# Weighing all edge chunks ahead of the slice softmax in a graph-attention gather loop, one core

## What is computed

```python
xn = layernorm(x)
h  = xn @ W.T + b                                   # graph attention
v  = leaky_relu(a1[src] + a2[dst])                  # one score an edge
ev = exp(v - segment_max(v, src)[src])
gnn = segment_sum((ev / segment_sum(ev, src)[src])[:, None] * h[dst], src)
mix = linear_attention(xn)                          # q / normaliser @ (k^T v) @ wo + bo
x = x + gnn + mix
y = layernorm(x)
sw = softmax((y @ W_x + b_x) @ W_slice / temp)      # 8 heads x 64 slices, a row a node
tok = sw^T @ (y @ W_fx + b_fx), normalised; attention over the 64 slice tokens
out = x + (attention output spread back by sw) @ W_out + b_out
```

## Time and profile before

| | us |
|---|---|
| median of 3 runs | 1620.71 |
| lowest and highest run | 1609.23, 1620.91 |
| span of the profiled execution, first to last instruction | 2306.1 |

### The profile page before, as it was taken

How to read it: one execution, slowest core, us unless ns; L and a number is a source line. 1 busy time by engine, 2 the same in 40 slices (tenths; PEclk the granted TensorE clock), 3 DMA queues, 4 the chain that set the end, 5 groups by cost and what they waited for, 6 DMA issues and landing times. The chain is left out here.

```text
span 2306.1 us, 27679 instructions
## 1 busy us (share of the span) xinstructions
PE 1454.6 (63%) x8420; PEld 1093.9 (47%) x8420; DVE 1270.9 (55%) x4043; ACT 677.9 (29%) x1884; POOL 1004.7 (44%) x1126
## 2 busy tenths in 40 slices
PE   5599995355745655655655656656646547465889
PEld 3477874234534434434434434434434435344667
DVE  8978783154644644644644545545545535445744
ACT  0243441042322322322322323323323323223310
POOL 1167676535445445445345345345344354453000
PEclk8799997577778877778878778778777777787999
DMA  8011213223223223223223222222232232221064
GB/s 178 29 47 48 62 50 90 71 58 88 70 70 87 69 69 86 69 73 84 68 73 83 68 76 80 68 77 79 65 83 77 62 87 68 69 77 55 14 193 153
DMA packets 112593, 177.17 MB, mean 77 GB/s; under 512 B 35998, under 2 KB 84509, under 8 KB 112445
## 3 DMA queue, kind: packets, MB, share of 16 engines
q0 software_dynamic: 43184, 109.96, 18.0%
q1 hardware_dynamic: 52847, 44.64, 7.5%
q10 hardware_dynamic: 16414, 20.81, 2.9%
HBM read 139.68 MB, written 35.65 MB: 76 GB/s over the span
## 5 line engine op out<-in xcount | busy, mean ns | idle before, releaser
L1134 POOL DMA_INDIRECT big<-node_table,rest x825 | 784.9, 951 | 239.9 <-issue 225.9
L1220 PE MATMUL psum<-big 128*125 128x257 f32 x1700 | 399.2, 388 | 39.4 <-DVE big L1757 39.1
L1220 PEld LDWEIGHTS psum<-big 128*125 128x125 f32 x1700 | 316.2, 191 | 93.9 <-DVE big L1757 46.1
L1575 DVE TENSOR_SCALAR rest<-psum,rest 128x125 f32<-128x125 f32 x100 | 30.1, 344 | 594.8 <-remote 554.1
L1239 PE MATMUL psum<-rest 65*125 65x512 bf16 x52 | 34.6, 666 | 488.6 <-ACT big L1376 488.6
L1132 POOL TENSOR_TENSOR rest<-rest 1x1 f32<-1x1 f32 x100 | 18.9, 189 | 693.7 <-PE psum L1220 668.0
L1370 ACT ACTIVATE rest<-big,rest 128x125 f32<-128x125 bf16 x850 | 268.9, 493 | 134.2 <-DVE rest L1705 134.2
L1239 PEld LDWEIGHTS psum<-rest 65*125 65x125 bf16 x52 | 9.2, 176 | 521.2 <-ACT big L1376 521.0
L1376 ACT COPY big<-psum 128x250 f32<-128x250 f32 x52 | 19.1, 367 | 687.1 <-remote 682.5
L1241 PE MATMUL psum<-rest,big 128*125 128x512 f32 x208 | 177.5, 1005 | 0.0
L1757 DVE TENSOR_SCALAR big<-big,rest 128x125 f32<-128x125 bf16 x850 | 169.0, 281 | 0.0
(11 more groups left out here) (430 smaller groups left out, 2786.7 us busy)
## 6 DMA issues: line engine op xcount, KB each, us to landing
big<-node_table,rest POOLq DMA_INDIRECT x825
slice_weights<-rest ACTq DMA_DIRECT2D x51, 252.0 KB
big<-slice_weights SPq DMA_DIRECT2D x50, 252.0 KB, 3.8
node_table<-big SPq DMA_DIRECT2D x50, 126.0 KB
normalised_turned<-big SPq DMA_DIRECT2D x50, 125.0 KB
rest<-normalised_turned SPq DMA_DIRECT2D x50, 125.0 KB
out_dram<-rest ACTq DMA_DIRECT2D x50, 125.0 KB
X<-in_x_dram SPq DMA_DIRECT2D x1, 5600.0 KB
```

The lines of the kernel that those rows point to most:

```text
L1134: pool.indirect_dma_start(Gt[:, u, q * TW:(q + 1) * TW], None, table, bass.IndirectOffsetOnAxis(ap=item[:, u, 2 * q:2 * q + 1], axis=0)).t ...
L1220: mm = pe.matmul(bank[bAgg][0:R, 0:D + 1], P[:, u, q, :], Gt[:, at, q * TW:q * TW + D + 1], start=q == 0, stop=q == Q - 1)
```

## The change

TensorE's step calls `sum_edges` once for all five groups of chunks; the two groups that stood behind `turn_weights` (5 of the 17 chunks) move ahead of `turn_inverse`. VectorE's `add_sums` is split into `take_sums` (the instruction that reads PSUM) and `invert_sums` (the three small ones). `weigh` moves ahead of `soft_below`, and `invert_sums` moves behind `inverse_norms`. Nothing else changes: the same instructions run, and ScalarE's and GpSimd's programs are as before.

```diff
@@ TensorE step @@
-                        sum_edges(i, u, odd, GROUPS[:3])
+                        sum_edges(i, u, odd, GROUPS)
                         turn_inverse(i + 1)
                         turn_weights(i)
-                        sum_edges(i, u, odd, GROUPS[3:])
                         spread_inverse(i + 1)
@@ VectorE @@
-                    def add_sums(i, done, count):
+                    def take_sums(i, done, count):
 
                         dve.wait_ge(done, count)
                         dve.scalar_tensor_tensor(AGG, AGG, keepf, bank[bAgg][0:R, 0:D + 1], ALU.mult,
                                                  ALU.add).then_inc(s_agg, 1)
+
+                    def invert_sums(i):
+
                         dve.wait_ge(s_agg, SA * i + 1)
                         dve.tensor_scalar(sinv, AGG[:, D:D + 1], 1e-30, None, ALU.max).then_inc(s_agg, 1)
@@ VectorE step @@
-                        add_sums(i, used[(u - 1) % U], n + 1 if u == 0 else n + 2)
+                        take_sums(i, used[(u - 1) % U], n + 1 if u == 0 else n + 2)
+                        weigh(i, u)
                         soft_below(i)
-                        weigh(i, u)
                         inverse_norms(i + 1, ahead)
+                        invert_sums(i)
                         if ahead:
                             scores(following_j, following_k, 1)
@@ VectorE, after the loop @@
-                    add_sums(last, used[(TAIL - 1) % U], 2 * more + (TAIL - 1) // U + 2)
+                    take_sums(last, used[(TAIL - 1) % U], 2 * more + (TAIL - 1) // U + 2)
+                    invert_sums(last)
```

## The result

| | us |
|---|---|
| changed kernel, median of 4 (lowest, highest) | 1745.69 (1745.15, 1745.94) |
| kernel before, median of 4 | 1616.43 (1609.23, 1620.91) |
| ratio, with 95% interval | 1.0815 [1.0769, 1.0862] |
| predicted | 1699, range 1631 to 1750 |

Slower, as forecast, and inside the range, but by 129 us where the sum had 78. The profiled execution of the changed kernel has a span of 1744.2 us, what the timed runs have. The profile of before had 2306.1.

The account below looks back on a forecast made before the run. No engine is full; a chain through several engines, about 20.5 us a step with GpSimd's gathers level, bounds the kernel. VectorE's 2.75 us delay less TensorE's 1.08, say 1.6 x 49 = 78 us, gives 1620.7 + 78 = 1699 us, range 1631 to 1750.

Parts of the forecast that it names:

- the sum: Whole loop: L1202 comes 1.7 and 1.5 us later, say 1.6, in each of 49 steps, 78 us.
- The wait at L1565: VectorE stands idle 2.7 us before L1565 for ScalarE's copies behind the late exponential; L1565 moves from 8.72 to 11.0.
- TensorE's series: TensorE's 34 matmuls, 7.8 us, run as one series from about 5 to about 13; L1202 then follows L1712 at once.
- Set-up and end taken over from the first profile: Set-up 474.3 us and end 143.0 us assumed equal in timed runs, leaving a 1003 us loop, 20.5 us a step.
- the hand-made 20.2 and 20.9: Clean step before the change: 20.2 us from the first step, 20.9 from the other with sums at 5.47; mean 20.5.
- its upper bound: Top of the range, 1750 us; all of VectorE's delay reaching the end was put at 49 x 2.75 = 135 us.
- Two signs that did not come: In the profile after: last L1742 intervals, without gathers, about 22.5 us; profiled span may move little, steps ending with gathers.
- 1, TensorE as the bound: Faster: the sums' earlier start wins up to 1.4 us a step, 69 us, giving 1552 us; chance 0.09.
- 2, another engine's pace: GpSimd's 20.5 us sets the pace and hides some delay: 1684 us, or 1631 at most for no change; chance 0.13.
- 3: Full delay: VectorE's small instructions ahead of `spread` late too, 1.1 us more; 49 x 2.75, 1756 us; chance 0.10.

Follow-up runs that it names:

- the run with the copies ahead: Changed kernel with ScalarE's three copies of the transposed marks moved ahead of the slice exponential: 1591.0 us, ratio to before 0.985.
- VectorE's part alone: Changed kernel with TensorE's sums put back into two series, the last five chunks behind the turning of the weights: 1815.3 us, ratio 1.122.
- the faster versions: Changed kernel with ScalarE's copies ahead of the exponential, 1591.0 us; that plus 3 filling matmuls, 1592.3; kernel before with 4 filling matmuls, 1591.9.
- TensorE's part alone: Kernel before with all 17 chunks summed ahead of the turning of the weights, VectorE's order as before: 1744.5 us in three runs, 1714.9 in the fourth.

## Why the prediction was right, and where it was short

- **The wait at L1565**: right within a tenth. Idle 2.7 us forecast, 2.74 measured; L1565's successor at 11.0 and 11.03; L1705's at 11.8 and 11.77; L1712's at 14.9 and 14.90; L1202 at 17.3 and 17.33. That the copies behind the exponential are the cause is shown by the run with the copies ahead, which takes it away.
- **TensorE's series**: "start at about 5 and are done by about 13", measured 4.77 and 12.37. L1202 follows L1714 at once (0.05 us). VectorE's part alone, where the five chunks stand in the way, shows what they cost: 1.4 us a step, the clock's part in it, against the 1.08 of the prediction.
- **Set-up and end taken over from the first profile**: at the pace of the timed runs set-up took 423.4 us, not 474.3, and what follows the last L1742 150.4, not 143.0. The first gathers already run in it, and what held TensorE up in the loop may have done so there (not shown). So before's step was 21.2 us, not 20.5; that 20.5 agreed with the hand-made 20.2 and 20.9 was luck, and hid that clean steps (20.4) stood beside longer ones (22.4).
- **The sum.** Clean steps: 22.2 (23.9 less 1.7) against 20.4, 1.8 us, 88 us over 49 steps (1.6 and 78 forecast). The clock: 1.7 us in every step of the changed kernel, 0.8 on average in before, net 0.9, 44 us. Together 132; measured 129. So a third of the loss is the clock, for which the sum had nothing; that the time still lies in the range is luck in so far, as its upper bound was drawn for the full delay of VectorE.
- **Two signs that did not come**: the last two intervals between L1744 were to be about 22.5 us and were 23.9 and 24.0, as the clock fell there too; the profiled span was to move little and went from 2306.1 to 1744.2, as the condition of the first profile was gone.
- **Rivals.** 1, TensorE as the bound: refuted for this change; with the copies ahead the same early weighing came out 1.5% ahead of before. 2, another engine's pace: GpSimd's gathers did stand level with the chain, and they are probably why the faster versions stop near 1591 us (argued, see above). 3 gave 1756 us, close to the measured time, but by small instructions of VectorE ahead of `spread`, which were not late; the agreement is chance.

## What to carry to other kernels

When work on one in-order engine is moved ahead of a result that another engine waits for, look at what that engine has queued behind the waiting instruction: here the exponential was not urgent, but three copies and nine products stood behind it, and swapping the copies ahead of it turned an 8% loss into a gain of 1.5%. A part that costs nothing in a hand-made sum can still cost TensorE its clock: where an edit leaves it waits of a microsecond or two in each step, count the stretch behind them at the lower level as a bound. Profile the kernel twice when its span and its timed runs disagree.

## What the runs showed of the hardware

- The clock fell behind waits of 1.0 to 2.1 us. In the changed kernel it did so in every step at the same place; in before, with a wait of 1.5 us, in 18 of 49 steps; in TensorE's part alone over the sums of nearly every step (10.17 us for 34 matmuls at 0.75), and one of its four runs was 30 us faster than the others. Idle TensorE filled with work that nobody reads gained 24 us for before, 67 for the changed kernel and 61 to 91 for TensorE's part.
- An indirect DMA of 128 rows holds GpSimd 1.25 us (0.95 and 0.30 between), 825 of them some 1035 us.
- The same kernel took 1607 to 1621 us in some jobs and 2279 to 2291 in another, and in the latter VectorE sees TensorE's signals only when GpSimd is nearly through with its gathers (a wait of 11.28 us in the step above).
